# Quantised attention: probabilities as bytes, transposed two keys at a time, with the bias made on GpSimd

## The reference, cut to what matters

```python
# x is (32, 64, 256), cond = ctx_2048 is (32, 64, 256): 2048 queries, 2048 keys, 16 heads of 16
H, hd = (NUM_HEADS, HEAD_DIM)
q = (x @ Wq + bq).reshape(1, B * N, H, hd)
kv = (cond @ Wkv + bkv).reshape(1, -1, 2, H, hd)
...
q = _fq_sym(q, axis=-1)          # round(x / s) * s, s = max|x| / 127
k = _fq_sym(k, axis=-1)
v = _fq_sym(v, axis=2)
attn = jnp.einsum('bhqd,bhkd->bhqk', q, k)
attn = jax.nn.softmax(attn.astype(jnp.float32), axis=-1)
attn = _fq_unsigned(attn, axis=-1)   # round(x / s) * s, s = max x / 255
out = jnp.einsum('bhqk,bhkd->bhqd', attn, v)
out = jnp.transpose(out, (0, 2, 1, 3)).reshape(B, N, C)
return out @ Wp + bp
```

## Time and profile before

| | us |
|---|---|
| time, median of 3 runs | 3039.45 |
| lowest and highest of the 3 | 3037.06, 3040.23 |
| the profiled execution: its own time | 3038.51 |
| span of its instructions in the trace | 3036.7 |
| first to last start of line 1682, in the loop of the change | 1655.9 to 2450.5 |
| VectorE busy in the span | 1932.5 |
| TensorE busy in the span | 2498.7 |
| ScalarE busy in the span | 1482.0 |
| GpSimd busy in the span | 409.3 |

### The profile page before, as it was taken

One profiled execution on the slowest core, in us unless ns is written; L12 is line 12 of the kernel. 1 busy time (PEld: TensorE's weight loads), 2 busy tenths in 40 slices (PEclk: granted clock), 3 DMA queues, 4 the chain that ended last, 5 costly groups with the idle time before them and its releaser, 6 DMA issues. The chain is left out here.

```text
span 3036.7 us, 50228 instructions
## 1 busy us (share of the span) xinstructions
PE 2498.7 (82%) x16570; PEld 1358.9 (45%) x16570; DVE 1932.5 (64%) x3686; ACT 1482.0 (49%) x2055; POOL 409.3 (13%) x454
## 2 busy tenths in 40 slices
PE   6874775999979999999664888787878865999998
PEld 3333554555547777777552222222222232444444
DVE  6995556667743333333456998888888845666665
ACT  5552332444433333333232776666666633666664
POOL 0001220111012222333133000000000001001100
PEclk9886776999979999999776555555555567999999
DMA  2000000000010000000000999999999940000001
GB/s 83 0 0 19 0 0 12 16 26 21 21 29 18 18 17 17 17 17 9 21 0 18 177 176 169 165 169 162 171 163 171 173 71 17 24 23 16 23 23 36
DMA packets 594876, 175.35 MB, mean 58 GB/s; under 512 B 548642, under 2 KB 594212, under 8 KB 594724
## 3 DMA queue, kind: packets, MB, share of 16 engines
q1 hardware_dynamic: 594724, 173.44, 29.6%
HBM read 37.07 MB, written 2.10 MB: 13 GB/s over the span
## 5 line engine op out<-in xcount | busy, mean ns | idle before, releaser
L1682 DVE TENSOR_SCALAR_CACHE_REDUCE ctxT<-psum,e_nsq 128x1024 f32<-128x1024 f32 x512 | 637.2, 1282 | 74.2 <-issue 54.1
L1651 PE MATMUL psum<-e_KT,e_Qs 48*128 48x512 bf16 x1024 | 519.9, 611 | 181.7 <-DVE ctxT L1682 151.0
L1703 ACT ACTIVATE xh<-ctxT,e_ebias 128x2048 uint16<-128x2048 f32 x128 | 256.2, 2002 | 134.0 <-DVE e_ebias L1686 134.0
L1703 ACT ACTIVATE xl<-ctxT,e_ebias 128x2048 uint16<-128x2048 f32 x128 | 256.2, 2002 | 119.2 <-DVE e_ebias L1686 119.2
L1651 PEld LDWEIGHTS psum<-e_KT,e_Qs 48*128 48x128 bf16 x1024 | 67.3, 104 | 415.8 <-issue 408.1
L103 PE MATMUL psum<-xh,d_WT 128*128 128x512 f16 x768 | 229.4, 381 | 2.6 <-DVE d_WT L1214 2.6
L1662 PEld LDWEIGHTS psum<-e_Vi,xnT 128*128 128x128 f16 x4096 | 129.5, 105 | 216.8 <-issue 216.8
L1233 DVE TENSOR_TENSOR d_ACC<-psum,d_ACC 128x512 f32<-128x512 f32 x128 | 82.5, 686 | 171.1 <-PE psum L1287 171.1
L103 PE MATMUL psum<-xh,f_WA 128*128 128x512 f16 x544 | 152.7, 383 | 13.9 <-DVEq L1896 11.8
L103 PE MATMUL psum<-xh,c_Wx 128*128 128x512 f16 x576 | 161.3, 383 | 0.8 <-DVE X L960 0.8
L1662 PE MATMUL psum<-e_Vi,xnT 128*128 128x16 f16 x4096 | 152.5, 175 | 8.1 <-DMA xnT<-xh 4.5
(11 more groups left out here) (312 smaller groups left out, 4965.9 us busy)
## 6 DMA issues: line engine op xcount, KB each, us to landing
d_Wn<-in_L_attn_w_qkv SPq DMA_DIRECT2D x16, 384.0 KB, 3.2
f_W<-in_L_ffn_w_routed SPq DMA_DIRECT2D x32, 176.0 KB, 2.5
ctx_rows<-in_ctx SPq DMA_DIRECT2D x1, 2048.0 KB, 8.6
X<-in_x SPq DMA_DIRECT2D x1, 2048.0 KB, 14.0
c_Wgu<-in_L_ffn_rg SPq DMA_DIRECT2D x16, 128.0 KB, 2.1
c_Wgu<-in_L_ffn_rw SPq DMA_DIRECT2D x16, 128.0 KB, 2.2
c_Wd<-in_L_ffn_rw SPq DMA_DIRECT2D x16, 128.0 KB, 2.2
d_Wn<-in_L_attn_w_gate SPq DMA_DIRECT2D x16, 128.0 KB, 3.0
```

What stands on the lines that cost most here:

```text
L1651: mm = pe.matmul(m.bank[b + q], Qs[rows, x.u // 2 % QSLOTS, :], KTt[rows, j // 2, (2 * hf + q) * BLK:(2 * hf + q + 1) * BLK], start=True, ...
L1682: dve.tensor_scalar(S32[:, sl, hf * HALF:(hf + 1) * HALF].rearrange("p (a b) -> p a b", a=2), m.psum[:, b:b + 2, :], nsq[:, ds(x.n(), 1)], ...
L1703: act.activation(e16[x.u % SLOTS], S32[:, x.u % 2, :], ACT.Exp, bias=ebias[:, x.u % 2:x.u % 2 + 1], scale=-1.0, accum_out=esum[:, ds(x.n() ...
```

## The change

Exponentials are written as uint8. The DMA transposes them as 1024 elements of 16 bits, so an element holds two neighbouring keys of a query, and its result goes to a new tile P8 in xl. GpSimd then casts the bytes to bfloat16 in PT, and takes the two keys apart while it does so: it reads 2048 bytes of a partition in order, and writes the two bytes of a pair 128 elements apart. Keys are laid out in KT so that the pairs fall into blocks as the values want them. GpSimd also makes ebias, which VectorE made before. S32, mn and ebias have 4 slots in place of 2. LAG is 7, the queries are fetched 4 pairs ahead, and the cast of a unit stands 3 units (LATE) behind its bias.

```diff
-        Vi = sb("Vi", [P, KT, H, HD], F16)
+        Vi = sb("Vi", [P, KT, H, HD], BF16)
...
-                            act.activation(KTt[:, :, ds(t * P, P)], m.bank[b + 1].bitcast(BF16)
-                                           .rearrange("p (a b) -> p a b", a=PR), ACT.Copy).then_inc(stored, 1)
+                            act.activation(KTt[:, :, ds(i * 2 * TPB * P + tt // 2 * 2 * P, 2 * P)]
+                                           .rearrange("p a (q b) -> p a q b", b=2)[:, :, :, tt % 2],
+                                           m.bank[b + 1].bitcast(BF16).rearrange("p (a b) -> p a b", a=PR),
+                                           ACT.Copy).then_inc(stored, 1)
...
-        BODY, SLOTS, LAG, QAHEAD, QSLOTS = 48, 4, 6, 3, 6
+        BODY, SLOTS, LAG, LATE, QAHEAD, QSLOTS = 48, 4, 7, 3, 4, 6
...
-        S32 = m.ctxT
-        PT = m.xnT[:, :, :].rearrange("p a b -> p (a b)").bitcast(F16).rearrange("p (s k q) -> p s k q", s=SLOTS, k=KT)
-        e16 = [x[:, :, :].rearrange("p a b -> p (a b)").bitcast(U16)[:, i * TOK:(i + 1) * TOK]
-               for x in (m.xh, m.xl) for i in range(2)]
+        S32 = [m.ctxT[:, 0, :], m.ctxT[:, 1, :], Smore[:, 0, :], Smore[:, 1, :]]
+        PT = m.xnT[:, :, :].rearrange("p a b -> p (a b)").bitcast(BF16).rearrange("p (s k q) -> p s k q", s=SLOTS, k=KT)
+        e8 = m.xh[:, :, :].rearrange("p a b -> p (a b)").bitcast(U8).rearrange("p (s k) -> p s k", s=SLOTS)
+        P8 = m.xl[:, :, :].rearrange("p a b -> p (a b)").bitcast(U16).rearrange("p (s c q) -> p s c q", s=SLOTS, c=KT // 2)
...
 # GpSimd
                 def step(x):
-                    if not x.exists():
-                        return
                     ahead = x.back(-2 * QAHEAD)
                     if x.u % 2 == 0 and ahead.exists():
                         fetch(ahead)
+                    if x.exists():
+                        m.wait_apart(pool, score_out, x.n(1, 2) + 2)
+                        sl = x.u % SLOTS
+                        pool.tensor_scalar(ebias[:, sl:sl + 1], mn[:, sl, 0:1], mn[:, sl, 1:2], LN255,
+                                           ALU.min, ALU.add).then_inc(biased, 1)
+                    if x.back(LATE).exists():
+                        unpack(x.back(LATE))
+
+                def unpack(x):
+                    m.wait_apart(pool, laid[x.u % SLOTS], x.n(SLOTS, 16) + 16)
+                    if x.at_least(SLOTS):
+                        m.wait_apart(pool, mixed, x.n() - (SLOTS - 1))
+                    pool.tensor_copy(PT[:, x.u % SLOTS, :, :].rearrange("p (c b) q -> p c q b", b=2),
+                                     P8[:, x.u % SLOTS, :, :].rearrange("p c q -> p (c q)").bitcast(U8)
+                                     .rearrange("p (c q b) -> p c q b", c=KT // 2, b=2)).then_inc(unpacked, 1)
...
 # SyncE
-                        m.wait_apart(sp, mixed, x.n() - (SLOTS - 1))
-                    sp.dma_start_transpose(PT[:, x.u % SLOTS, :, :], e16[x.u % SLOTS].bitcast(F16)).then_inc(laid[x.u % SLOTS], 16)
+                        m.wait_apart(sp, unpacked, x.n() - (SLOTS - 1))
+                    sp.dma_start_transpose(P8[:, x.u % SLOTS, :, :], e8[:, x.u % SLOTS, :].bitcast(U16)).then_inc(laid[x.u % SLOTS], 16)
...
 # TensorE, mix
-                    m.wait_apart(pe, laid[x.u % SLOTS], x.n(SLOTS, 16) + 16)
+                    m.wait_apart(pe, unpacked, x.n() + 1)
...
 # VectorE
-                    sl = x.u % 2
-                    if x.at_least(2):
-                        m.wait_apart(dve, exped, x.n() - 1)
+                    sl = x.u % SLOTS
+                    if x.at_least(SLOTS):
+                        m.wait_apart(dve, exped, x.n() - (SLOTS - 1))
...
-                    m.wait_apart(dve, score_out, x.n(1, 2) + 2)
-                    dve.tensor_scalar(ebias[:, sl:sl + 1], mn[:, sl, 0:1], mn[:, sl, 1:2], LN255,
-                                      ALU.min, ALU.add).then_inc(biased, 1)
...
 # ScalarE
-                        act.activation(e16[x.u % SLOTS], S32[:, x.u % 2, :], ACT.Exp, bias=ebias[:, x.u % 2:x.u % 2 + 1],
+                        act.activation(e8[:, x.u % SLOTS, :], S32[x.u % SLOTS], ACT.Exp, bias=ebias[:, x.u % SLOTS:x.u % SLOTS + 1],
```

More of the change, by code:

```diff
@@ L1375, in quantised_attention @@
     chain_s, vmaxed, vall = (m.sem(f"e_{n}") for n in ("chain", "vmax", "vall"))
-    q_here, scored, score_out, biased, exped, mixed, normed, chain2 = (m.sem(f"e_{n}") for n in (
-        "q_here", "scored", "score_out", "biased", "exped", "mixed", "normed", "chain2"))
+    q_here, scored, score_out, biased, exped, unpacked, mixed, normed, chain2 = (m.sem(f"e_{n}") for n in (
+        "q_here", "scored", "score_out", "biased", "exped", "unpacked", "mixed", "normed", "chain2"))
     laid = [m.sem(f"e_laid{i}") for i in range(4)]
@@ L1556, in quantised_attention @@
         N = NT * H
-        BODY, SLOTS, LAG, QAHEAD, QSLOTS = 48, 4, 6, 3, 6
+        BODY, SLOTS, LAG, LATE, QAHEAD, QSLOTS = 48, 4, 7, 3, 4, 6
         Qs = sb("Qs", [P, QSLOTS, P], BF16)
-        mn = sb("mn", [P, 2, 2])
-        ebias = sb("ebias", [P, 2])
+        mn = sb("mn", [P, SLOTS, 2])
+        ebias = sb("ebias", [P, SLOTS])
         esum = sb("esum", [P, N])
         Osb = sb("Osb", [P, NT, D])
-        S32 = m.ctxT
-        PT = m.xnT[:, :, :].rearrange("p a b -> p (a b)").bitcast(F16).rearrange("p (s k q) -> p s k q", s=SLOTS, k=KT)
-        e16 = [x[:, :, :].rearrange("p a b -> p (a b)").bitcast(U16)[:, i * TOK:(i + 1) * TOK]
-               for x in (m.xh, m.xl) for i in range(2)]
+        Smore = sb("Smore", [P, 2, TOK])
+        S32 = [m.ctxT[:, 0, :], m.ctxT[:, 1, :], Smore[:, 0, :], Smore[:, 1, :]]
+        PT = m.xnT[:, :, :].rearrange("p a b -> p (a b)").bitcast(BF16).rearrange("p (s k q) -> p s k q", s=SLOTS, k=KT)
+        e8 = m.xh[:, :, :].rearrange("p a b -> p (a b)").bitcast(U8).rearrange("p (s k) -> p s k", s=SLOTS)
+        P8 = m.xl[:, :, :].rearrange("p a b -> p (a b)").bitcast(U16).rearrange("p (s c q) -> p s c q", s=SLOTS, c=KT // 2)
         class Unit:
@@ L1622, in step @@
                         fetch(ahead)
+                    if x.exists():
[12 more added lines that the diff above has]
+                                     .rearrange("p (c q b) -> p c q b", c=KT // 2, b=2)).then_inc(unpacked, 1)
                 for p in range(QAHEAD):
                     fetch(Unit(0, 2 * p))
-                loop(pool, step)
+                loop(pool, step, LATE)
             @block.sync
@@ L1681, in step @@
                         m.wait_apart(dve, scored, x.n(1, 2) + hf + 1)
-                        dve.tensor_scalar(S32[:, sl, hf * HALF:(hf + 1) * HALF].rearrange("p (a b) -> p a b", a=2),
+                        dve.tensor_scalar(S32[sl][:, hf * HALF:(hf + 1) * HALF].rearrange("p (a b) -> p a b", a=2),
                                           m.psum[:, b:b + 2, :], nsq[:, ds(x.n(), 1)], None, ALU.mult, ALU.min,
                                           accum_out=mn[:, sl, hf:hf + 1]).then_inc(score_out, 1)
-                    m.wait_apart(dve, score_out, x.n(1, 2) + 2)
-                    dve.tensor_scalar(ebias[:, sl:sl + 1], mn[:, sl, 0:1], mn[:, sl, 1:2], LN255,
-                                      ALU.min, ALU.add).then_inc(biased, 1)
                 loop(dve, step)
@@ L1695, in output @@
                     act.activation(Osb[:, ds(x.n(H), 1), half * P:(half + 1) * P].rearrange("p a b -> p (a b)"),
-                                   m.bank[6 + half][:, 0:P], ACT.Copy, scale=2.0 ** 24).then_inc(normed, 1)
+                                   m.bank[6 + half][:, 0:P], ACT.Copy).then_inc(normed, 1)
                 def step(x):
```

## The result

| | before | changed |
|---|---|---|
| time, median, us | 3038.26 (4 runs, 3036.92 to 3040.23) | 4731.63 (4 runs, 4728.33 to 4731.95) |
| ratio of the times | | 1.557, 95% interval 1.5543 to 1.5597 |
| profiled execution, us | 3038.51 | 4731.75 |
| loop of the quantised attention, us | 805 (1655.9 to 2461.1) | 2496 (1655.1 to 4150.7) |

The changed kernel takes 1.56 times as long. Nearly all of it is in the loop, measured from VectorE's first half to the end of the last copy of outputs: 1690 us more there, 1693 in the whole execution. The forecast was 2906 us, in a range to 3235, so the result lies far outside.

The account below looks back on a forecast made before the run. VectorE was taken to bound the loop at 3.10 us a unit, with DMA as full. 256 x 2.54 + 13.2 = 663.4 us in place of 795.9 saved 132.5 from 3038.5: 2906 us, range 2865 to 3235.

Parts of the forecast that it names:

- 2.91 as the upper bound: Cast on GpSimd: 0.183 + 1.706 x 1.6 us, the factor 1.60 coming from VectorE's strided reduce.
- Rival A: Cast, line 1636: scattered writes make GpSimd the bound; at 2.91 us a cast, time 3085 to 3195 us; chance 0.29.
- The bound of before: Attention loop before the change: VectorE waits for nobody, its halves starting 1.21 and 1.89 us apart, together 3.10 a unit.
- at most 0.1 us a unit: Loop: the most that taking the bias off VectorE alone could give, with the DMA engines as full.
- DMA as a second full resource: Loop before the change: DMA engines 96.8% busy, so one transpose takes 3.0 us of them.
- VectorE's floor of 2.42: Loop without biases on VectorE: two halves, 1.21 us apart, leave at least 2.42 us a unit.
- TensorE's and ScalarE's below it: Loop: TensorE needs at most 2.48 us a unit, ScalarE 2.0 plus 0.03, so neither was taken as the bound.
- four slots enough: S32 in the loop: VectorE waits for the exponential four units back, not two, which covers a bias that comes later.
- rival B's lock: VectorE's reduces slow GpSimd's cast to 3.7 us, time near 3290 us; chance 0.10 together with slow bytes.
- The bias 0.18: GpSimd in the loop: the bias, one element, costs about a copy's fixed 0.18 us.
- The middle of 2.42 and 2.65: Loop period taken as 2.54 us, because GpSimd waits for another engine before every bias and every cast.
- A's cheaper form: Scattered cast at 2.91 us, GpSimd period 3.24 to 3.67, time 3085 to 3195 us; the other form had a factor of 2.

Follow-up runs that it names:

- the second kernel of copies: Kernel before with 18 timed copies added at its start, on GpSimd, VectorE and ScalarE; GpSimd lines cost 1.8 ns in whole words, 4.4 ns in part words.
- the one in good order: Changed kernel with the cast reading every second byte and writing in order: 2888.93 us, ratio 0.9513 to the kernel before.

## Why the prediction was wrong, point by point

- *The step that failed: the cast.* "The trace has no cast of bytes and no write that jumps" was true. I took the price of writes in order, 1.89 us, as the value and 2.91 as the upper bound, and the cast took 9.22. Rival A named the place and the mechanism, GpSimd as the bound through scattered writes, and its signs came true one by one: ScalarE, TensorE and VectorE wait in the end for lines 1627 and 1636, and GpSimd is busy nine tenths. But its price was wrong in two ways. I took the strided reduce as a factor of 1.60 and applied it to GpSimd's 0.83 ns an element. The runs fit a time for each line better: 1.70 ns for that reduce, and nearly the same, 1.75, for GpSimd's strided read in the second kernel of copies, which is 2.1 times its price in order. That gives 0.18 + 2048 x 1.70 = 3.7 us, not 2.9. And a write of part of a word costs 4.4 ns a line, which no row of before bounded. The casts then start 9.70 us apart, which makes 2483 of the loop's 2496 us.
- *The arguments against A*: "a write need not be waited for" did not help, since scattered writes cost more here (4.4 ns) than scattered reads (1.75). And "GpSimd is slower than VectorE to begin with" misreads the rows: 0.83 ns an element is less than the 1.06 of VectorE's reduce.
- *The bound of before* (VectorE, 1.21 and 1.89): right. Moving the bias, with four slots, freed 90 us, and putting it back took all of the gain. The "at most 0.1 us a unit" for moving it without halving the transposes was too little: it was 0.35, for the reason in the next point.
- *DMA as a second full resource*: wrong in size. I took 96.8% busy for a capacity of 3.0 us a transpose. They came every 2.73 us when the bias was off VectorE. Bytes are still worth 59 us behind the bias (2948 to 2889).
- *VectorE's floor of 2.42, TensorE's and ScalarE's below it, four slots enough, no contention on the fetch*: right, by the kernel without a cast and by the one in good order. There the exponential of bytes took 2.00 us and the cast ran at 1891 ns beside VectorE's halves, so rival B's lock did not happen. The fetch took 296 ns there; its 524 in the changed kernel were mostly overlap with the end of the slow cast.
- *The bias 0.18*: it was 0.29. The fixed cost of a copy was not that of this operation. It cost about 0.1 us a unit.
- *The middle of 2.42 and 2.65*: for a cast of 1.89, the sum gave 2906 and 2889 was measured. GpSimd's period was 2.45 in steady work, not 2.54: it seldom waited before a bias or a cast.
- *The Trainium skill*, "SBUF — State Buffer", section on the DMA port swizzle, had the line of 16 bytes and a penalty for leaving it, and the copies agree with it: the price follows the number of such lines (4.42 and 4.43 ns each). It also says that two hits in a line are enough for full bandwidth. There the measurement decides otherwise: GpSimd's bfloat16 writes with four elements in a line took 2450 ns and with two 4716, against 1893 in order. The Trainium skill's factor for reads, in "GPSIMD Engine Reference", section 7, would have given 2.74 us for the cast, an estimate; for writes of parts of words the runs show 9.22, and for GpSimd's reads 16 bytes apart a factor of 2.1.
- *The chances*: I gave 0.39 to A and B together and cut the range at A's cheaper form. The cast occurs 256 times on one engine and the trace didn't show its price, so each microsecond of error in it moved the time by 256. The range should have stayed open above.

## What to carry to other kernels

When a copy must take elements apart, let the write run in order and let the read jump: here that was one line and 1843 us, with a read of every second byte. Reads with larger steps are not free either (1.75 ns an element at 16 bytes on GpSimd). Where a trace shows a stride penalty, try it as a time for each 16-byte line that is reached and not only as a factor on another engine's rate. On GpSimd, count lines with writes of less than four bytes 2.5 times. A queue that serves both a long piece and a short one that others wait for needs slots enough for the long one: here four in place of two were worth 114 us. A DMA share near 100% is not yet a limit.

## What was not expected of the hardware

- The same scattered cast costs as much on ScalarE (9216 ns) as on GpSimd (9197), and 5310 on VectorE, against 1909, 1891 and 1226 in order.
- A milder case was in the changed kernel all along: the copy of keys on ScalarE, now with steps of 4 bytes, took 1313 ns a tile in place of 1018. ScalarE waits for TensorE there, and the loop starts no later.
- Two streams of reads that take turns cost far less than such writes: 2117 ns for 2048 bfloat16, 2048 bytes apart (line 185 of the second kernel).
